# Another order for first norms, weight loads, table look-ups and first gathers in a four-layer graph network kernel on one Trainium2 core

## What is computed

```python
edge_index = stack([src, dst])
x = layernorm(x + L0(x, node_vec, edge_weight, edge_attr_128, ...))   # attention over edges, with a cosine time code
x = layernorm(x + L1(x, ...))    # three graph convolutions scaled by degree, with side paths
x = layernorm(x + L2(x, edge_attr_128, src, dst, ...))   # two rounds of mean messages and self weights
x = layernorm(x + L3(x, edge_attr_2, src, dst, ...))     # attention over two edge features
```

## Time and profile before

| | |
|---|---|
| median of 3 runs | 3533.83 us (3531.9 to 3536.51) |
| the profiled execution | 3541.67 us, of which the span is 3539.8 us |
| busy share of the span | PE 68%, DVE 67%, ACT 57%, POOL 60% |
| DMA | 678.87 MB, 192 GB/s over the span |

### The profile page before, as it was taken

How to read it: one execution, slowest core, us unless ns; L and a number is a source line. 1 busy time by engine, 2 the same in 40 slices (tenths; PEclk the granted TensorE clock), 3 DMA queues, 4 the chain that set the end, 5 groups by cost and what they waited for, 6 DMA issues and landing times. The chain is left out here.

```text
span 3539.8 us, 54325 instructions
## 1 busy us (share of the span) xinstructions
PE 2391.4 (68%) x13252; PEld 1807.2 (51%) x13252; DVE 2366.0 (67%) x7373; ACT 2033.0 (57%) x6253; POOL 2122.5 (60%) x2026
## 2 busy tenths in 40 slices
PE   6757772599966776774577677666656657777430
PEld 4523331466645555553466566545446657776330
DVE  6669991244458869987466677699834459978442
ACT  5624441567731159997577777789834448875110
POOL 7737773277600048773677577577577767710776
PEclk9979996599978888887788788877778879987555
DMA  6735555577719954553577788789778689943231
GB/s 183 207 106 154 156 152 112 165 241 247 239 54 285 297 169 165 171 171 126 172 232 221 231 267 264 241 265 285 228 228 224 196 228 277 265 128 105 84 91 41
DMA packets 521816, 678.87 MB, mean 192 GB/s; under 512 B 98910, under 2 KB 285669, under 8 KB 521504
## 3 DMA queue, kind: packets, MB, share of 16 engines
q1 hardware_dynamic: 455202, 549.18, 50.0%
q0 software_dynamic: 65856, 125.82, 13.5%
q10 hardware_dynamic: 446, 0.40, 0.0%
HBM read 398.69 MB, written 280.39 MB: 192 GB/s over the span
## 5 line engine op out<-in xcount | busy, mean ns | idle before, releaser
L1495 POOL DMA_INDIRECT xg<-r_d,src_row x392 | 426.3, 1087 | 170.0 <-issue 115.5
L1495 POOL DMA_INDIRECT xg<-x_d,src_any x392 | 415.1, 1059 | 154.2 <-issue 116.7
L1829 POOL DMA_INDIRECT look<-table_d,ids x196 | 202.1, 1031 | 360.2 <-DVEq L1784 303.7
L2885 POOL DMA_INDIRECT out<-x_f,out_row x196 | 203.0, 1036 | 176.8 <-DVE x_f L2951 118.0
L1128 POOL DMA_INDIRECT xd<-in_x,ids x196 | 216.0, 1102 | 73.2 <-issue 51.1
L1495 POOL DMA_INDIRECT xg<-g_d,src_any x196 | 200.6, 1024 | 79.3 <-issue 52.1
L718 POOL DMA_INDIRECT rows_d<-row,slot_i x196 | 193.5, 987 | 69.5 <-issue 56.7
L2259 ACT ACTIVATE term_c<-xg,scale 128x128 f32<-128x128 f32 x392 | 125.3, 395 | 149.7 <-DMA xg<-r_d,src_row 71.4
L2611 ACT ACTIVATE term_c<-term_c,inv_deg 128x128 f32<-128x128 f32 x392 | 124.9, 392 | 130.8 <-DVE term_c L2627 130.7
L2225 PE MATMUL m_ps_c<-w_L_gnn_Wr,term_t_c 128*128 128x128 f32 x784 | 129.6, 317 | 104.2 <-ACT m_c L2250 104.2
L2171 DVE TENSOR_TENSOR_SCAN agg_t_c<-flags_c,agg_t_c,t_ps_c 128x512 f32<-128x512 bf16 x144 | 183.4, 1274 | 3.9 <-PE t_ps_c L2553 3.8
(11 more groups left out here) (510 smaller groups left out, 8407.4 us busy)
## 6 DMA issues: line engine op xcount, KB each, us to landing
flags_c<-cont_d SPq DMA_DIRECT2D x245, 128.0 KB
xm<-rows_d SPq DMA_DIRECT2D x49, 512.0 KB
m_d<-m_c SPq DMA_DIRECT2D x98, 256.0 KB, 4.4
r_d<-r_c SPq DMA_DIRECT2D x98, 256.0 KB
m_in_c<-m_d SPq DMA_DIRECT2D x98, 256.0 KB
x_c<-x_d SPq DMA_DIRECT2D x98, 256.0 KB, 4.3
e_c<-rows_d SPq DMA_DIRECT2D x98, 256.0 KB
g_d<-g_f SPq DMA_DIRECT2D x50, 258.0 KB
```

Source lines behind the costliest of these rows:

```text
L1495: pool.indirect_dma_start(out=xg[:, n % SC, k, 0:width], out_offset=None, in_=table, in_offset=bass.IndirectOffsetOnAxis(ap=rows[:, t:t + ...
L1829: pool.indirect_dma_start(out=look[:, t, :], out_offset=None, in_=table_d[:, :], in_offset=bass.IndirectOffsetOnAxis(ap=ids[:, 0, t:t + 1] ...
L2885: pool.indirect_dma_start(out=out[:, :], out_offset=bass.IndirectOffsetOnAxis(ap=out_row[:, t:t + 1], axis=0), in_=x4[:, n % SF, k, :], in ...
```

## The change

It has five parts. (1) In the early pipeline ScalarE's step is reordered: scaled rows of q-3 come ahead of the copy of q and the squares of q-1. (2) In the counting stage the bound on stores no longer follows the number of loads but the gathered groups. (3) In the ranking stage the 47 weight loads are issued in 49 shares, one behind each group's row loads. (4) In the flag stage the first four x loads are issued ahead of the record loads. (5) The first 32 of the 196 look-ups move to the line stage, which now has a GpSimd program that ends with a wait for them, and the seven first gather groups of the node stage are issued one per step from step NG + 3 on, behind the same waits.

```diff
+        LOOKED = 32
+
+        def look_up(pool, t):
+
+            pool.indirect_dma_start(
+                out=look[:, t, :], out_offset=None, in_=table_d[:, :],
+                in_offset=bass.IndirectOffsetOnAxis(ap=ids[:, 0, t:t + 1], axis=0),
+                bounds_check=TABLE - 1, oob_is_err=False).then_inc(looked.sem, 16)
...
@@ early_act: after root of q - 2
+            j = q - 3
+            if lo <= j < hi:
+                act.wait_ge(p_inv.sem, p_inv.at(j + 1))
+                if j >= FO:
+                    act.wait_ge(p_out[j % FO].sem, p_out[j % FO].at(j // FO))
+                for k in range(K):
+                    made = act.activation(x1_p[:, j % FO, k, :], nm[j % FM][:, chunk(k)], ACT.Copy, scale=inv_p[:, j % 2, k:k + 1])
+                made.then_inc(p_rows.sem, 1)
...
@@ early_act: after squares of q - 1
-            j = q - 3
-            if lo <= j < hi:
-                act.wait_ge(p_inv.sem, p_inv.at(j + 1))
...
-                made.then_inc(p_rows.sem, 1)
...
@@ counting stage, SyncE
-                        while stored < loaded - FX - 3:
+                        while stored < min(loaded, (i + 1) * PACE // 100 - 5):
...
@@ ranking stage, SyncE, inside the loop over groups
-                    for to, w in to_load:
-                        sp.dma_start(to, w).then_inc(weights_in.sem, 16)
+                        for to, w in to_load[len(to_load) * g // GROUPS:len(to_load) * (g + 1) // GROUPS]:
+                            sp.dma_start(to, w).then_inc(weights_in.sem, 16)
...
@@ flag stage, SyncE
+                    for j in range(COUNTED, COUNTED + FX):
+                        early_load(sp, j)
                     for k in range(K):
                         sp.dma_start(recs[:, k::K, :], rows_d[:, 2 * D:ROW].rearrange("(n p k) f -> p k n f", p=P, k=K)[:, k, :, :]).then_inc(once_in.sem, 16)
-                    for j in range(COUNTED, COUNTED + FX):
-                        early_load(sp, j)
...
@@ line stage
+                @block.gpsimd
+                def _(pool):
+                    for t in range(LOOKED):
+                        look_up(pool, t)
+                    pool.wait_ge(looked.sem, looked.at(LOOKED))
...
@@ node stage, dense_pool
-                    for t in range(TILES * (it - 1) // LOOKS, TILES * it // LOOKS):
-                        pool.indirect_dma_start(
...
+                    for t in range(LOOKED + (TILES - LOOKED) * (it - 1) // LOOKS, LOOKED + (TILES - LOOKED) * it // LOOKS):
+                        look_up(pool, t)
...
@@ node stage, GpSimd
+                    ahead = 0
                     for it in range(NG + LAG):
                         dense_pool(pool, it)
-                    pool.wait_ge(rows_found.sem, rows_found.at(1))
-                    for s in range(2):
-                        pool.wait_ge(s_out[s].sem, s_out[s].at(len(range(s, NG, 2))))
-                    for n in range(AHEAD_1):
-                        gather_group(pool, n, x1_d[:, :], SLOTS + N, src_any, D)
+                        if it == NG + 3:
+                            pool.wait_ge(rows_found.sem, rows_found.at(1))
+                            for s in range(2):
+                                pool.wait_ge(s_out[s].sem, s_out[s].at(len(range(s, NG, 2))))
+                        if it >= NG + 3 and ahead < AHEAD_1:
+                            gather_group(pool, ahead, x1_d[:, :], SLOTS + N, src_any, D)
+                            ahead += 1
```

More of the change, by code:

```diff
@@ L334, in early_act @@
                 made.then_inc(p_squared.sem, 1)
-            j = q - 3
-            if lo <= j < hi:
-                act.wait_ge(p_inv.sem, p_inv.at(j + 1))
-                if j >= FO:
-                    act.wait_ge(p_out[j % FO].sem, p_out[j % FO].at(j // FO))
-                for k in range(K):
-                    made = act.activation(x1_p[:, j % FO, k, :], nm[j % FM][:, chunk(k)], ACT.Copy, scale=inv_p[:, j % 2, k:k + 1])
-                made.then_inc(p_rows.sem, 1)
         def early_dve(dve, j):
@@ L1304, in graph_kernel @@
             weighed = signal("weighed")
+            looked = signal("looked", 16, "pool_queue")
             w_turned, w_made = signal("w_turned"), signal("w_made")
@@ L1536, in graph_kernel @@
             lanes_made, lanes_up, lanes_down = signal("lanes_made"), signal("lanes_up"), signal("lanes_down")
-            looked = signal("looked", 16, "pool_queue")
             x_in = [signal(f"x_in{s}", 16) for s in range(6)]
@@ L1827, in dense_pool @@
                     pool.wait_ge(spread_ok.sem, spread_ok.at(it))
-                    for t in range(TILES * (it - 1) // LOOKS, TILES * it // LOOKS):
-                        pool.indirect_dma_start(
-                            out=look[:, t, :], out_offset=None, in_=table_d[:, :],
-                            in_offset=bass.IndirectOffsetOnAxis(ap=ids[:, 0, t:t + 1], axis=0),
-                            bounds_check=TABLE - 1, oob_is_err=False).then_inc(looked.sem, 16)
+                    for t in range(LOOKED + (TILES - LOOKED) * (it - 1) // LOOKS, LOOKED + (TILES - LOOKED) * it // LOOKS):
+                        look_up(pool, t)
             with ExitStack() as ps, nc.Block() as block:
```

## The result

The kernel after takes 3455.91 us (median of 4 runs, 3453.19 to 3459.22), the kernel before 3535.17 us beside it (median of 4): ratio 0.9774, 95% interval 0.9758 to 0.9789, 79.3 us faster. Two places gained where the forecast had nothing: the node stage's look-ups, and convolutions 4 and 5.

A forecast was written before the change was run, and what follows sets the result against it. No engine was taken to bound the whole kernel; limits change by stage. Gains of 22.1 counting, 9.7 ranking, 21.6 flags, -9.6 line and 12.7 node sum to 56.5 us, giving 3477.3 us, range 3459 to 3495.

The forecast's parts named there:

- The stall: Counting stage: VectorE idle while ScalarE's scaling waits for an x_d store; the new store bound was to gain 18.5 us.
- the order: Counting stage: scaling ahead of copy and squares frees TensorE's bank earlier; gain 3.6 us, bounds 0 and 7.
- no ScalarE wait on a store: Sign of being right, counting stage: ScalarE would never wait there for a store, as stores land in 3.0 us.
- TensorE waiting for ScalarE's copy: Sign of being wrong: TensorE held by ScalarE's copy, which stands behind a wait for a store.
- Rival 3: Early pipeline: a store's landing of 3.0 us enters each of 50 steps, +150 us, ending near 3643; chance 0.02.
- Rival 4: Ranking stage: weights between rows delay GpSimd, 19 us lost in place of 9.7 gained, 3506; chance 0.04.
- I take 3.8 (between 3.42 and 5.13, ...): Flag stage: nine steps from the sixth block on fall from 5.13 to 3.8 us each, gaining 12.0 us.
- Rival 1: Counting and flag stages: the new order gives nothing; total gain 40.9 us, 3493; chance 0.13.
- I take 9.3, since two of the three say so: Line stage: 9.3 us for landing and drain after GpSimd's look-ups, making the stage 9.6 us longer.
- Rival 2: Line stage: GpSimd and VectorE shut each other out, loss 40 us, total gain 26, 3507; chance 0.04.
- What it buys, 5 look-ups per step becoming 4, I put at nothing: Node stage: fewer look-ups per step gain 0 us, because VectorE and ScalarE set the step.
- The gathers: End of node stage: 16 gathers and not 28 stand behind the last multiply; gain 12.7 us, bounds 8 and 15.6.

The follow-up runs named there:

- runs 1 and 2: Kernel before with one edit each: 1, the new store bound in the counting stage, 3516.73 us; 2, ScalarE's new row order, 3513.00 us.
- Runs 3 and 4: Kernel after with one part undone each: 3, no look-ups in the line stage, 3462.17 us; 4, node stage's first gathers behind all steps, 3466.97 us.
- run 16: Kernel after with 28 look-ups in the line stage, not 32, and the first gather groups from step NG + 2 on: 3445.95 us.
- run 6: Kernel after, unchanged, measured again among the long executions: 4102.58 us, ratio 0.9878.

## Why the prediction was right and wrong

**Counting, right in size; a sign failed.** The stall went whole. Of the 22.1 forecast, 18.5 were the stall and 3.6 the order; the runs say 20.5 and 2.6. The 2 us above the stall may be the restart of TensorE that I had left open; no run separates it. I had held ScalarE's wait for a store to be met, since three steps are about 10 us and a store lands in 3.0, and named "no ScalarE wait on a store" as a sign. There are thirteen, 28.2 us in all, and "TensorE waiting for ScalarE's copy", one of my signs of being wrong, is there with 10.0 us. They come with the order (runs 1 and 2). Rival 3 is true in small; what these waits cost is only known to have left 2.6 us of gain.

**Ranking, right** in place and size (10.8 for 9.7). SyncE's slack covered the weights: from barrier to last scatter 347.8 us before and 347.2 after. Rival 4 falls. It was priced too low: the 47 issues took not 0.4 us each but 41 us together before, from 544.46 to 585.6.

**Flags, mechanism right, a term mis-sized.** Up to the sixth block the stage gave 8.1 us of the 9.6 forecast. The step "I take 3.8 (between 3.42 and 5.13, ...)" failed: the nine steps took 3.13 us each, which is 18.0 us and not 12.0; another 1.3 came behind the fifteenth step. I had bounded the step by TensorE's time at the lower clock, but the granted clock did not stay there: over the nine steps its mean was 0.91, and in the stretches at 1.00 ScalarE's 2.87 us is the bound. With the order alone the steps gave 16.3 us. Rival 1 falls.

**Line stage, sign right, a term mis-sized.** "I take 9.3, since two of the three say so": the loss was 6.4. The wait ended 1.6 us after the last look-up and the drain took 2.66. I had taken drains of other stages as if the drain were a constant. With 28 look-ups in the block it takes 2.33 us, with 32 it takes 2.66: 0.083 us each. Rival 2 falls: the look-ups in the line stage took at most 1.29 us. The Trainium skill's "SBUF — State Buffer", section "SBUF: two separate sides", has VectorE operations with two SBUF inputs and GpSimd operations that read SBUF exclude each other for a whole instruction. This trace does not show that of indirect DMAs, 32 of which passed beside 30 us of VectorE work, some 19 of them in operations with two or more input tiles, with 1.34 us from one to the next.

**Node stage, a step failed.** "What it buys, 5 look-ups per step becoming 4, I put at nothing: in the node stage VectorE and ScalarE set the step." Until the first product GpSimd set the pace, with 28 look-ups 1.30 us apart: four or five fewer brought it 5.6 us earlier (41.9 and 36.3 us in the mean of the ordinary executions). In full run the sentence was nearly right, since 5, 5 and 4 look-ups need 7.28 us a step against 7.30; there the gain is 302.3 - 299.0 = 3.3 us in the mean, less than such a count moves by itself. (The long executions have more: 309.7 us with none moved, two of them, against 299.8, ten.) Then the node stage's own drain got shorter: 24.71 us to 22.10 with the same 12 gathers still to come, 2.6 us for 32 fewer DMAs, again 0.08 each. The gathers gave some 13 us, as forecast (12.7). Against the three profiles of the old node code (440.3, 445.6, 444.4; mean 443.4) the stage gained 25.0: 5.3 ahead of the first product, about 4 in the steps, 2.6 in the drain and 13. The profile that I forecast from had the shortest of the three.

**Untouched stages.** Convolutions 4 and 5 took 579.7 to 583.4 us in three profiles without the whole change and 574.5 to 576.9 in five with most of it, some 6 us less. Runs 3 and 4 leave the look-ups and the gathers out as its cause, run 1 and 2 the two counting edits. Of the other two parts no ordinary execution alone was had. This is left open, and I found nothing in the code that links them. With these 6 us back the time would have been 3462, inside the range; so would it without the 8 us that the node stage gained ahead of the first product and in its drain.

**The sum.** To the 56.5 forecast come the node steps and drain (5.7 and 2.6 in this pair of profiles, by the product of step NG + 3, which started 376.2 and then 370.5 us into the stage; 5.2 of the 5.7 lie ahead of the first product), the flag steps and head (5.9), the line stage (3.2), ranking, counting and gathers (3) and the unexplained 6.5: 83, against the 82.5 of the two spans; the other untouched stages make up the rest. All corrections but two of 1 us (the flag head, the order in counting) have the same sign. In the line stage that is caution; for the rest no reason is shown, and it may be chance. The range was also added up wrong: "Its own terms at their bounds reach from about 3460 to 3493", but 18.5 + 7 + 11 + 9.6 + 19 - 2.5 + 15.6 = 78.2 us gives 3455.6, and 18.5 + 0 + 9.6 - 12 + 8 = 24.1 gives 3509.7. The measured time lies just inside these bounds.

## What to carry to other kernels

Where a queue's work is spread over the steps of a pipeline, price it apart for the fill and for the full run: here the look-ups set the pace ahead of the first product and, in the ordinary executions, cost little behind it, where steps with four made good what steps with five lost. Spread what an idle queue can carry, but count the drain that the new work leaves at the stage's end. An order that frees one wait can bring another, so look for the wait it moves ahead of other work. And where TensorE stands at its lower clock in a stage that the change relieves, work the step out at both levels. When a range is built from bounds, add the bounds up.

## What the runs showed of the hardware

- In two stages the GpSimd drain at a block's end grows with the indirect DMAs issued in it: in the line stage 2.33 us for 28 and 2.66 for 32, paid though GpSimd has waited for all of them, and in the node stage 2.6 us less for 32 fewer. It is no price that holds in every stage: the ranking stage, with some 260, has 6.91 us. In run 16:

```profile
L1316 POOLq DRAIN  x1: 2331/2331/2331, 1004.6 to 1004.6; - x1
```

- Four loads of 32-byte pieces hold SyncE's issue for 10.6 to 12.7 us, and then the next load for 3.6: what is urgent goes ahead of them.
- In twelve runs all kernels took 4050 to 4165 us with nearly the same busy time on VectorE, ScalarE and GpSimd (2364 against 2362 us on VectorE). The profile puts the difference down to idle time that it marks "remote", ended by nothing of this core. The gains of the flag and node stages stayed, the counting stage's could not be seen in it.

The largest of them in run 6, as the waits of the whole span show it (sum, count, longest):

```profile
DVE agg_t_c L2186 <- remote: 320.7, 43, 39.6
...
ACT slope_c L2599 <- remote: 183.0, 25, 39.1
...
ACT term_t_c L2259 <- remote: 159.6, 32, 11.0
```
